# First score passes of an attention stage inside the last feed forward, constant rows loaded once per lot, and some causal masks added by TensorE

## Chip, cores and metric

The kernel runs on one core of a Trainium2 chip. The metric is device time in microseconds (us) of one execution, the median of several runs.

## What is computed

The reference takes x of shape (16, 256, 128), float32, and adds six blocks to it one after the other, each on a layer norm of x:

```python
x = x + 0.5 * ffn0(layernorm(x))      # gated: silu(x w1) * (x w2), two 512x512 gelu layers, 512 -> 128
x = x + attn0(layernorm(x))           # no softmax: (theta phi^T / sqrt(128)) g
x = x + 0.5 * ffn0(layernorm(x))      # the same weights again
x = x + 0.5 * moe(layernorm(x))       # 8 experts, top 2, chosen by each sequence's first row
x = x + attn1(layernorm(x))           # 16 heads of width 8, RoPE, causal softmax over 256 positions
x = x + 0.5 * moe(layernorm(x))
```

## The kernel before, in words

**Order.** All instructions of all engines come from one list of steps. The class `Order` lays it out before the program is built: jobs (generators) call `put` for a step once its inputs are ready by the planned clocks of the engines. `TAKES` (from line 62) holds the planned microseconds of each step on each engine (P TensorE, V VectorE, A ScalarE, G GpSimd, S the sync queue, D a DMA's flight). Among the jobs that can go on, the one with the smallest priority number goes first, and `SHIFT` adds a small number to single jobs. Each engine then runs its steps in the order of the list and waits for semaphores. All DMAs are issued by the SP queue, also in the order of the list.

**Work before the softmax attention.** x is cut into 8 chunks of 512 rows (c = 0 to 7), and the 16 feed forwards (two for each chunk, `QUEUE`) run in two streams, `stream(0)` and `stream(1)`, whose matmuls TensorE takes in turn (`term`, lines 1000 and 1004: a high and a low half of the activations, float32 rounded, 128x512 each). Between the layers ScalarE does silu or gelu (L1457, L1461) and the rounding to the high half (L1468), and VectorE the product (L1292) and the low half (L1297). A stream that finds the queue empty is dead. The first stream to die frees the SBUF that buffers 0 to 2 of the attention use, the second frees the rest: `order.dead` holds their last `down` steps, and `ffns_dead` makes an engine wait for them. In the last feed forward only one stream is alive.

**Preparation.** After a chunk's second feed forward and its experts (`first_moe`), `prepare` turns q and k (L1407, L1411), splits each into three bf16 parts on ScalarE and GpSimd, and `spread` writes them to DRAM (L1669). There are 16 sequences u, two to a chunk. `attend` puts the step `reloc`: SP loads K and Q of a sequence into buffer u % 5 (`KS`, `QS`, L1700). Four rows of each half of KS and two of QS are constants, loaded once (L1690), and `VA` gets a constant pattern (L1686); these loads are the step `ones`, put by the job `opening` (priority 4).

**Attention.** For each sequence there are 8 groups of two heads. `pass1` (job `peaks`) is 4 mask matmuls (L1179) and 4 score matmuls (L1183, L1186) into a pair of PSUM banks, and then one VectorE maximum over 128x768 (L1414). After 8 of them the row maxima are combined (`peak`, L1421), transposed, copied to `MT` (L1427) and sent by SP into two rows of QS (`max_out`, L1705). Then `pass2` (job `probs`) is 4 matmuls (L1213), one exponential over 128x768 on ScalarE (L1553) and one `affine_select` on GpSimd that zeroes the masked half (L1643), and `weigh` multiplies the probabilities by the values (L1227). `fin`, a second `moe` and the stores follow. `probs` starts only when both streams are dead, since its buffer `PB` lies where their data lay. The priority of `peaks` is 5.5 while pass1 is less than `LEAD` = 20 steps ahead of pass2, and 6.5 then; pass2 has 6, the streams 3, their endings 2.85, the work after them 2. `pair` gives a pair of banks only if the planned clock of the reading engine is less than `QUEUED` = 1.0 us ahead of TensorE's. Where the plan shows TensorE idle, `keep` (L1197) fills in small matmuls whose result nobody reads.

Of the kernel before, what the change touches and what calls it, by code (L numbers as in the profile page):

```python
# [7 lines left out]
F32 = mybir.dt.float32  # L8
# [7 lines left out]
S = 256  # L16
# [14 lines left out]
class Step:  # L31
# [68 lines left out]
WEIGH = 6.5  # L100
KEPT = 5
SLOTS = 8
QUEUED = 1.0
LEAD = 20
LONE = 4.0
FILLED = 0.65
# [5 lines left out]
SHIFT = {  # L112
    ("attend", 0): -0.23, ("attend", 1): 0.32, ("attend", 2): -0.07, ("attend", 3): 0.31, ("attend", 11): -0.03,
    ("attend", 12): 0.09, ("attend", 13): 0.54, ("attend", 14): 0.12,
    ("fin", 0): 0.1, ("fin", 4): -0.75, ("fin", 9): -0.69, ("fin", 12): 0.02, ("fin", 14): 0.51,
    ("lone", 7): -0.03,
    ("maxima", 1): -0.03, ("maxima", 4): -0.05, ("maxima", 6): -1.07, ("maxima", 7): -0.15, ("maxima", 8): 0.18,
    ("maxima", 9): 0.02, ("maxima", 12): 0.91, ("maxima", 13): 0.14, ("maxima", 14): 0.54, ("maxima", 15): 0.88,
    ("peaks", 0): -0.31, ("peaks", 4): 0.27, ("peaks", 5): -0.02, ("peaks", 6): 0.13, ("peaks", 7): -0.15,
    ("peaks", 8): -0.11, ("peaks", 9): 0.34, ("peaks", 11): -0.52, ("peaks", 13): -0.26, ("peaks", 15): -0.16,  # L120
    ("probs", 0): 0.09, ("probs", 3): -0.01, ("probs", 5): -0.03, ("probs", 6): -0.39, ("probs", 8): 0.02,
    ("probs", 9): 0.25, ("probs", 10): 0.03, ("probs", 12): 0.24, ("probs", 14): -0.2,
    ("weigher", 0): -0.23, ("weigher", 3): -0.12, ("weigher", 4): 0.01, ("weigher", 8): -0.52,
    ("weigher", 15): -0.24,
}
# [33 lines left out]
class Order:  # L159
# [37 lines left out]
    def put(self, name, **k):  # L197
# [19 lines left out]
        if name == "up" and not self.opened:  # L217
            late = "up_first"
        for i, (eng, us, *way) in enumerate(TAKES[late]):
            if eng == "D":  # L220
                t += us
                continue
            if eng == "P":
                kind = TILES.get(name, "f")
                self.clock["P"] += 0.094 * (kind != self.pe)
                self.pe = kind
            if eng == "A":
                table = "gelu" if name == "tanh" and self.table == "silu" else TABLES.get(name, self.table)
                self.clock["A"] += 1.29 * (table != self.table)
                self.table = table  # L230
            if i or name == "up":
                t = max(t, later - 0.45 * (name == "up"))
            s0 = max((ready if name in BESIDE else t) + HOPS[eng], self.clock[eng])
            if eng == "P":
                self.fill(s0)
                self.idle_from = s0 + us
            self.note(eng, s0, s0 + us, name)
            self.clock[eng] = s0 + us
            t = st.at[eng] = s0 + way[0]
# [55 lines left out]
    def pair(self, eng):  # L295
        while True:
            for b in (4, 2, 0):
                if self.clock[eng] < self.clock["P"] + QUEUED and self.bank[b] is not None and self.bank[b + 1] is not None and self.left(self.bank[b] + self.bank[b + 1]) <= self.clock["P"] + AHEAD:
                    return b
            yield  # L300
# [51 lines left out]
    def next_feed(self, s):  # L352
        if not self.queue:
            return None
        box = {"ffn": self.queue.pop(0)}
        self.add(1, self.begin(box) if box["ffn"] == QUEUE[0] else self.feed(s, box))
        return box
# [5 lines left out]
    def stream(self, s):  # L363
        box = self.next_feed(s)
        while box:
# [67 lines left out]
            self.bank[b] = None  # L433
            self.add(2.85, self.ending(p, c, b, mm))
        if self.first is None:
# [3 lines left out]
    def ending(self, p, c, b, mm):  # L439
        _, free = yield from self.yr.get(self)  # L440
        y = self.put("y", c=c, b=b, src=mm, emptied=free)
        self.bank[b] = [y]
        yield from self.until(y.done)
        b, free = yield from self.sr.get(self)
        bk = self.put("back", c=c, b=b, emptied=free, src=y)
        self.sr.free[b] = [bk]
        self.yr.free[0] = [bk]
        self.add(2, self.first_moe(c, bk) if p else self.attn0(c, bk))

# [69 lines left out]
    def prepare(self, c, src):  # L519
# [31 lines left out]
        for h in range(2):  # L551
            self.add(2.5, self.attend(2 * c + h, a, va), of=("attend", 2 * c + h))
        if c >= NC - 2:
# [22 lines left out]
    def opening(self):  # L576

        for n in range(KEPT):
            m = 1 if n < 3 else 2
            while len(self.dead) < m:  # L580
                yield
            yield from self.until(self.dead[m - 1].done)
            if m == 2:
                self.sr.ids = [6, 7, 5, 4]
            self.qfree[n] = [self.dead[m - 1]]
            self.vfree[n] = [self.put("ones", i=n, x=m, src=self.dead[m - 1])]

    def attend(self, u, prep, va):
# [5 lines left out]
        self.turn["reloc"] += 1  # L594
        self.add(self.lead, self.peaks(u, rl), "h", ("peaks", u))
        while self.vfree[u % KEPT] is None:
# [34 lines left out]
    def probs(self, u, mx):  # L631
# [4 lines left out]
        for i in range(8):  # L636
            while self.pbfree[i % SLOTS] is None:
                yield
            k = yield from self.pair("A")
            p2 = self.put("pass2", u=u, g=i, b=k, src=mx, emptied=self.bank[k] + self.bank[k + 1],  # L640
                          emptied2=self.pbfree[i % SLOTS])
# [91 lines left out]
    def lay(self):  # L733
        self.add(lambda: self.rank(0), self.stream(0))
        self.add(lambda: self.rank(1), self.stream(1))
        self.add(4, self.opening())
        self.run()
# [14 lines left out]
def build(nc, I, out):  # L752
    order = Order()
    with ExitStack() as ctx:
# [81 lines left out]
        QS, KS, VA = {}, {}, {}  # L836
        for n in range(KEPT):
            QS[n] = sb(f"QS{n}", [128, 8, S], BF16)
            KS[n] = sb(f"KS{n}", [128, 8, S], BF16)
            VA[n] = sb(f"VA{n}", [128, 2, NH, 32])  # L840
        PB = sb("PB", [128, SLOTS, 3, 2, 128])
# [13 lines left out]
        s_one = [sem(f"s_one{u}") for u in range(KEPT)]  # L855
        s_far = [sem(f"s_far{u}") for u in range(KEPT)]
        s_qs = [sem(f"s_qs{u}") for u in range(KEPT)]
# [53 lines left out]
        for st in order.steps:  # L911
            if st.name == "down" and st.x:
                k += 1
                nth_down[id(st)] = k


# [81 lines left out]
        def tensor(e, w, steps, lo):  # L998
# [7 lines left out]
            for st in steps:  # L1006
# [163 lines left out]
                elif st.name == "pass1":  # L1170
                    K, Q = KS[u % KEPT], QS[u % KEPT]
                    w.wait_ge(s_qs[u % KEPT], 64 * (u // KEPT + 1))
                    w.wait_ge(s_far[u % KEPT], 64)
                    w.wait_ge(g_c, 6)
# [31 lines left out]
                elif st.name == "pass2":  # L1206
# [3 lines left out]
                    for k in range(2):  # L1210
                        for h in range(2):
                            o = PSA[:, b + h, 0:384].rearrange("p (t q) -> p t q", t=3)
                            t = e.matmul(o[:, 1, :] if k else o[:, 0::2, :],  # L1213
                                         K[64 * h:64 * h + 52, g, 128 * k:128 * k + 128],
                                         Q[64 * h:64 * h + 52, g, 128 * k:256], start=(k == 0), stop=True,
                                         skip_group_check=True)
                    t.then_inc(p_pass2, 1)
                elif st.name in ("weigh", "weighed"):

                    V, a = VA[u % KEPT], g % 2  # L1220
                    w.wait_ge(g_sel, 8 * u + 2 * g + 2)
                    w.wait_ge(a_vexp, u + 1)
# [350 lines left out]
        def gpsimd(e, w):  # L1573
# [4 lines left out]
            for st in order.steps:  # L1578
# [58 lines left out]
                elif st.name == "rest1":  # L1637
                    w.wait_ge(a_cast, 2 * n + 2)
                    e.tensor_tensor(CB[:, g, 2, :], RA[:, 0, :], CB[:, g, 1, :], ALU.subtract).then_inc(g_rest, 1)
                elif st.name == "pass2":  # L1640
                    P = PB[:, n % SLOTS, 0:2, :, :].rearrange("p t l q -> p (t l) q")
# [4 lines left out]
        def sync(e, w):  # L1646
# [25 lines left out]
            for st in order.steps:  # L1672
# [10 lines left out]
                elif st.name == "ones":  # L1683
# [3 lines left out]
                        s_one[st.i], 16)  # L1687
                    for T, a, z in ((KS, 0, 4), (QS, 4, 6)):
                        for h in range(2):
                            e.dma_start(T[st.i][64 * h + 48:64 * h + 48 + z - a, :, :].rearrange(  # L1690
                                "p g s -> p (g s)").bitcast(F32), I["rows"][a:z, :]).then_inc(s_far[st.i], 16)
                elif st.name == "reloc":
                    for side in range(2):
                        w.wait_ge(s_dk[c % 2][side], n_dk * (c // 2 + 1))
                    for s in st.emptied:
                        if s.name == "pass2":
# [108 lines left out]
```

## Time and profile before

| what | value |
|---|---|
| median of 3 runs | 651.84 us (649.85 to 653.08) |
| the profiled execution: its time, its span | 652.16 us, 650.4 us |
| busy share of the span: PE, PEld, DVE, ACT, POOL | 95%, 72%, 75%, 75%, 47% |

PE is TensorE's matmuls, PEld its weight loads, DVE VectorE, ACT ScalarE, POOL GpSimd, SPq the sync engine's DMA issue. Spans of matmuls are modelled and overlap, so a busy PE is not PE at its peak. Idle time of an engine that is not the bottleneck costs nothing. The profile gives for each idle time the instruction whose semaphore came last.

### The profile page before, as it was taken

The numbers are of one execution on the slowest core, as the hardware profiler recorded it, in microseconds if no ns is written. First come the engines' busy times: TensorE is split into PE (matmuls) and PEld (weight loads), VectorE is DVE, ScalarE is ACT, GpSimd is POOL, SyncE is SP. The second block draws the span as 40 slices with busy tenths as digits, with TensorE's granted clock in tenths as the row PEclk, the third lists the DMA queues.
The fourth block names the chain that finished last, engine by engine and source line by source line (L and its number), as shares of the span: only waits on it lengthen the run. The fifth ranks groups of instructions, "written<-read, shape, count | busy, mean of one in ns | idle before, by whom it ended". The sixth has DMA issues, their size and how long they took to land.

```text
span 650.4 us, 14027 instructions
## 1 busy us (share of the span) xinstructions
PE 615.8 (95%) x5210; PEld 466.2 (72%) x5210; DVE 487.3 (75%) x1262; ACT 485.6 (75%) x816; POOL 306.1 (47%) x476
## 2 busy tenths in 40 slices
PE   4899999999999999999999999988999999999997
PEld 3677878888887887888778887765555666656665
DVE  6767566675675777675978768799988989888846
ACT  5799778787887687787788777724777857877892
POOL 1402202321311525222638354576888766767683
PEclk9899999999999999999999999999999999999999
DMA  9300000000000002100002035454444323122002
GB/s 290 109 1 1 1 0 2 1 2 1 1 1 2 0 2 58 40 1 1 1 26 72 2 90 154 155 165 144 122 122 139 113 81 112 55 90 89 10 3 68
DMA packets 41886, 37.80 MB, mean 58 GB/s; under 512 B 2940, under 2 KB 37020, under 8 KB 41816
## 3 DMA queue, kind: packets, MB, share of 16 engines
q1 hardware_dynamic: 41816, 36.87, 18.4%
q8 instruction: 43, 0.70, 0.4%
q14 instruction: 27, 0.22, 0.1%
HBM read 21.92 MB, written 14.68 MB: 56 GB/s over the span
## 4 chain that ended last, share of the span: by engine, by line
PE 66%; DVE 14%; ACT 9%; issue 5%; DMA 2%; POOL 2%; SPq 1%; DVEq 0%; ACTq 0%; POOLq 0%
PE PSA L1000 20%; PE PSA L1004 20%; PE PSA L1227 6%; DVE MX L1414 3%; PE PSA L1019 3%; DVE G L1292 3%; PE PSA L1213 3%; PE PSA L1179 2%; ACT PSA L1461 2%; PE PSA L1156 2%; DMA QS<-MT 2%; ACT G L1457 1%; PE PSA L1163 1%; PE PSA L1186 1%; PE PSA L1197 1%
## 5 line engine op out<-in xcount | busy, mean ns | idle before, releaser
L1000 PE MATMUL PSA<-ah,WH 128*128 128x512 f32 x320 | 130.3, 407 | 0.5 <-DVE G L1292 0.5
L1414 DVE TENSOR_REDUCE MX<-PSA 128x6 f32<-128x768 f32 x128 | 117.9, 949 | 13.8 <-PE PSA L1186 13.1
L1461 ACT ACTIVATE PSA<-PSA,SC 128x512 f32<-128x512 f32 x128 | 84.7, 662 | 55.0 <-PE PSA L1004 54.4
L1004 PE MATMUL PSA<-al,WH 128*128 128x512 f32 x320 | 125.4, 392 | 0.0
L1553 ACT ACTIVATE PB<-PSA 128x768 f32<-128x768 f32 x128 | 98.6, 813 | 28.9 <-PE PSA L1213 27.6
L1000 PE MATMUL PSA<-bh,WH 128*128 128x512 f32 x256 | 104.8, 410 | 2.7 <-DVE G L1292 2.3
L1583 POOL TENSOR_SCALAR VE<-MV 128x4 f32<-128x4 f32 x46 | 11.4, 247 | 194.4 <-DVE MV L1267 194.4
L1004 PE MATMUL PSA<-bl,WH 128*128 128x512 f32 x256 | 100.3, 392 | 0.0
L1643 POOL TENSOR_SCALAR_AFFINE_SELECT PB<-PB 128x512 f32<-128x512 f32 x128 | 80.2, 636 | 36.0 <-ACT PB L1553 34.0
L1297 DVE TENSOR_TENSOR al<-PSA,ah 128x512 fp32r<-128x512 f32 x64 | 44.0, 687 | 52.7 <-ACT ah L1468 52.2
L1000 PEld LDWEIGHTS PSA<-ah,WH 128*128 128x128 f32 x320 | 60.5, 189 | 13.3 <-issue 0.7
L1297 DVE TENSOR_TENSOR bl<-PSA,bh 128x512 fp32r<-128x512 f32 x64 | 44.0, 687 | 33.7 <-ACT bh L1468 33.4
L1004 PEld LDWEIGHTS PSA<-al,WH 128*128 128x128 f32 x320 | 60.5, 189 | 12.1 <-issue 0.7
L1292 DVE SCALAR_TENSOR_TENSOR G<-PSA,SC,G 128x512 f32<-128x512 f32 x64 | 46.7, 747 | 29.6 <-ACT G L1457 22.8
L1597 POOL TENSOR_SCALAR XN<-X,MV,RS 128x128 f32<-128x128 f32 x78 | 62.8, 814 | 3.1
L1000 PEld LDWEIGHTS PSA<-bh,WH 128*128 128x128 f32 x256 | 48.1, 188 | 14.1 <-DVE G L1292 4.9
L1227 PE MATMUL PSA<-PB,VA 128*32 128x256 f32 (+1 forms) x1024 | 55.3, 337 | 2.3 <-DVE X L1317 0.9
L1004 PEld LDWEIGHTS PSA<-bl,WH 128*128 128x128 f32 x256 | 48.2, 188 | 8.9 <-issue 0.2
L1000 PE MATMUL PSA<-XH,WH 128*128 128x512 f32 x128 | 53.3, 416 | 1.4 <-DVE XL L1287 1.4
L1004 PE MATMUL PSA<-XL,WH 128*128 128x512 f32 x128 | 51.1, 399 | 0.0
L1468 ACT ACTIVATE ah<-G 128x512 fp32r<-128x512 f32 x64 | 40.4, 631 | 12.8 <-DVE G L1292 12.7
L1585 POOL TENSOR_TENSOR RS<-VE,MHALF 128x4 f32<-128x4 f32 x46 | 47.9, 1042 | 3.8
(163 smaller groups left out, 1282.7 us busy)
## 6 DMA issues: line engine op xcount, KB each, us to landing
KS<-dk SPq DMA_DIRECT2D x32, 192.0 KB
QS<-dq SPq DMA_DIRECT2D x32, 192.0 KB
dk<-CB SPq DMA_DIRECT2D x16, 192.0 KB, 2.3
dq<-CB SPq DMA_DIRECT2D x16, 192.0 KB, 2.5
VA<-in_ones SPq DMA_DIRECT2D x5, 512.0 KB, 4.7
X<-in_x SPq DMA_DIRECT2D x8, 256.0 KB, 6.8
dk<-CB SPq DMA_DIRECT2D x16, 128.0 KB, 2.0
dq<-CB SPq DMA_DIRECT2D x16, 128.0 KB, 1.9
```

Source lines behind the costliest of these rows:

```text
L1000: e.matmul(o, WH[:, col:col + 128], hi, start=first, stop=False)
L1004: return e.matmul(o, WH[:, col:col + 128], low, start=False, stop=last)
L1227: t = e.matmul(PSA[32 * v:32 * v + 32, b, 128 * k:256], V[:, k, 8 * (g // 2) + 2 * v + a, :], P[:, 1, :] if k else P[:, 0::2, :], start=(k ...
L1292: e.scalar_tensor_tensor(out=G[:, i, :], in0=bank(b), scalar=SC[:, 4 + st.j:5 + st.j], in1=G[:, i, :], op0=ALU.mult, op1=ALU.mult).then_in ...
L1297: e.tensor_tensor(cut(PL_[st.s, dst], st.j), h, cut(PH_[st.s, dst], st.j), ALU.subtract).then_inc(v_lo, 1)
L1414: e.tensor_reduce(MX[:, u % 2, 1:4, :].rearrange("p t (l g) -> p l t g", l=2)[:, :, :, g], PSA[:, b:b + 2, 0:384].rearrange("p l (t k) -> ...
L1461: e.activation(bank(b), bank(b), ACT.Gelu, scale=SC[:, k:k + 1]).then_inc(a_gelu, 1)
L1468: e.activation(cut(PH_[st.s, dst], st.j), G[:, i, :] if g == 0 else bank(b), ACT.Copy).then_inc(a_hi, 1)
L1553: e.activation(PB[:, n % SLOTS, :, :, :].rearrange("p t l q -> p l t q"), PSA[:, b:b + 2, 0:384].rearrange("p l (t q) -> p l t q", t=3), A ...
L1585: e.tensor_tensor(RS[:, i, :], VE[:, i, :], MHALF[:, :], ALU.pow).then_inc(g_rs, 1)
L1597: t = e.tensor_scalar(XN[:, i, j, :], X[:, 4 * c + j, :], MV[:, i, j, 0:1], RS[:, i, j:j + 1], ALU.subtract, ALU.mult)
L1643: e.affine_select(out=P, in_=P, compare_op=ALU.is_ge, fill=0.0, base=0, pattern=[[0, 4], [1, 128]], channel_multiplier=-1).then_inc(g_sel, 1)
```

## The change

`opening` gets priority 1 in place of 4 and works by lots: buffers 0 to 2 when the first stream is dead, 3 and 4 when both are. It puts a new step `rows` first: four DMAs that load the constant rows of all buffers of the lot, from a source repeated by a zero stride (so K and Q of a lot now lie in one tensor `KQ`). The loads into `VA` (`ones`) come after the lot's last `reloc`. `reloc` waits for the dead streams itself. `attend` gets priority 1 in place of 2.5. The job `peaks` of sequences 0 to 2 gets priority 1.5, ahead of the streams, and while fewer than two streams are dead `pair` allows 2.0 us in place of 1.0. A `pass2` is of kind "m" if the planned clock of GpSimd is more than `BEHIND` = 2.0 us ahead of TensorE's: then four more matmuls add the mask (−1e30) to the scores before the exponential, and there is no `affine_select`. `feed`, `ending` and the work after it become jobs that `SHIFT` can name, and all numbers of `SHIFT` are others.

```diff
-    "value": ..., "ones": [("S", 2.4, 2.4), ("D", 6.0)],
+    "value": ..., "rows": [("S", 1.2, 1.2), ("D", 2.0)], "ones": [("S", 0.4, 0.4), ("D", 5.5)],
+    "pass2m": [("P", 0.28, 0.45), ("A", 0.69, 0.81)],
...
+LOTS = (range(3), range(3, KEPT))
-QUEUED = 1.0
+QUEUED = (2.0, 1.0)
+FIRST = (3, 1.5)
+BEHIND = 2.0
...
-                if self.clock[eng] < self.clock["P"] + QUEUED and ...
+                if self.clock[eng] < self.clock["P"] + QUEUED[len(self.dead) > 1] and ...
...
-            self.add(2.5, self.attend(2 * c + h, a, va), of=("attend", 2 * c + h))
+            self.add(1, self.attend(2 * c + h, a, va), of=("attend", 2 * c + h))
...
     def opening(self):
-        for n in range(KEPT):
-            m = 1 if n < 3 else 2
+        for m, lot in ((1, LOTS[0]), (2, LOTS[1])):
             while len(self.dead) < m:
                 yield
             yield from self.until(self.dead[m - 1].done)
             if m == 2:
                 self.sr.ids = [6, 7, 5, 4]
-            self.qfree[n] = [self.dead[m - 1]]
-            self.vfree[n] = [self.put("ones", i=n, x=m, src=self.dead[m - 1])]
+            self.put("rows", i=m - 1, x=m, src=self.dead[m - 1])
+            for n in lot:
+                self.qfree[n] = [self.dead[m - 1]]
+            while self.turn["reloc"] <= lot[-1]:
+                yield
+            for n in lot:
+                self.vfree[n] = [self.put("ones", i=n, x=m, src=self.dead[m - 1])]
...
-        self.add(self.lead, self.peaks(u, rl), "h", ("peaks", u))
+        self.add(FIRST[1] if u < FIRST[0] else self.lead, self.peaks(u, rl), "h", ("peaks", u))
...
+            m = "m" if self.clock["G"] > self.clock["P"] + BEHIND else ""
-            p2 = self.put("pass2", u=u, g=i, b=k, src=mx, ...
+            p2 = self.put("pass2", u=u, g=i, b=k, kind=m, src=mx, ...
...
-        self.add(4, self.opening())
+        self.add(1, self.opening())
...
-        for n in range(KEPT):
-            QS[n] = sb(f"QS{n}", [128, 8, S], BF16)
-            KS[n] = sb(f"KS{n}", [128, 8, S], BF16)
-            VA[n] = sb(f"VA{n}", [128, 2, NH, 32])
+        for k, lot in enumerate(LOTS):
+            KQ[k] = sb(f"KQ{k}", [128, len(lot), 2, 8, S], BF16)
+            for i, n in enumerate(lot):
+                KS[n], QS[n] = KQ[k][:, i, 0, :, :], KQ[k][:, i, 1, :, :]
+                VA[n] = sb(f"VA{n}", [128, 2, NH, 32])
...
# tensor, pass2 (the four score matmuls then end with stop=st.kind != "m")
+                    if st.kind == "m":
+                        for k in range(2):
+                            for h in range(2):
+                                o = PSA[:, b + h, 0:256].rearrange("p (t q) -> p t q", t=2)
+                                t = e.matmul(o[:, :, 64 * k:64 * k + 64], MK[64 * h:64 * h + 64, k, 0, :],
+                                             IM[64 * h:64 * h + 64, k, 64 * k:64 * k + 64].rearrange(
+                                                 "p (o q) -> p o q", o=1).to_broadcast([64, 2, 64]),
+                                             start=False, stop=True, skip_group_check=True)
# tensor, weigh (chosen counts the affine_selects up to a pass2)
-                    w.wait_ge(g_sel, 8 * u + 2 * g + 2)
+                    w.wait_ge(a_prob, 8 * u + 2 * g + 2)
+                    w.wait_ge(g_sel, chosen[8 * u + 2 * g + 1])
# gpsimd
-                elif st.name == "pass2":
+                elif st.name == "pass2" and st.kind != "m":
# sync
-                    for T, a, z in ((KS, 0, 4), (QS, 4, 6)):
+                elif st.name == "rows":
+                    ffns_dead(w, st.x)
+                    for k, a, z in ((0, 0, 4), (1, 4, 6)):
                         for h in range(2):
-                            e.dma_start(T[st.i][64 * h + 48:64 * h + 48 + z - a, :, :].rearrange(
-                                "p g s -> p (g s)").bitcast(F32), I["rows"][a:z, :]).then_inc(s_far[st.i], 16)
+                            T = KQ[st.i][64 * h + 48:64 * h + 48 + z - a, :, k, :, :].rearrange(
+                                "p n g s -> p n (g s)").bitcast(F32)
+                            e.dma_start(T, I["rows"][a:z, :].rearrange("p (o s) -> p o s", o=1).to_broadcast(
+                                [z - a, len(LOTS[st.i]), 4 * S])).then_inc(s_far[st.i], 16)
                 elif st.name == "reloc":
...
+                    ffns_dead(w, 1 + (u % KEPT in LOTS[1]))
```

## Rows read from the trace of the kernel before

**Rows 1.** Windows: length, busy us of PE, PEld, DVE, ACT, POOL, clock, DMA.
```profile
393.00:425.00 32.00, 31.73 (x189) 24.95 (x188) 25.55 (x78) 24.02 (x41) 16.52 (x24) 1.00 0.53 170
425.00:450.00 25.00, 19.92 (x258) 13.45 (x256) 24.01 (x62) 6.27 (x14) 16.49 (x26) 1.00 0.51 159
450.00:617.50 167.50, 160.12 (x2543) 101.25 (x2539) 149.38 (x341) 123.75 (x230) 123.65 (x203) 0.99 0.31 95
617.50:640.00 22.50, 21.42 (x289) 14.21 (x285) 12.56 (x58) 18.59 (x36) 17.37 (x32) 1.00 0.05 14
```

**Rows 2.** The same windows, line L1414 (pass1's maxima) alone.
```profile
393.00:425.00 32.00, 1.90 (x2) 1.00 0.53 170
425.00:450.00 25.00, 13.26 (x15) 1.00 0.51 159
```

**Rows 3.** Groups of instructions, 450 to 617.5 us: busy, mean of one | idle before, releaser.
```profile
L1414 DVE TENSOR_REDUCE MX<-PSA 128x6 f32<-128x768 f32 x112 | 103.3, 949 | 13.8 <-PE PSA L1186 13.1
...
L1643 POOL TENSOR_SCALAR_AFFINE_SELECT PB<-PB 128x512 f32<-128x512 f32 x110 | 68.9, 636 | 33.2 <-ACT PB L1553 31.9
...
L1227 PEld LDWEIGHTS PSA<-PB,VA 128*32 128x32 f32 x880 | 24.2, 110 | 19.9 <-issue 7.3 <-POOL PB L1643 3.6
```

**Rows 4.** Timeline of the SP queue: start, us, line, DMAs.
```profile
393.83 0.69 SPq L1690 DMA_DIRECT2D KS<-in_rows  x2
394.56 0.54 SPq L1690 DMA_DIRECT2D QS<-in_rows  x2
...
398.97 1.65 SPq L1700 DMA_DIRECT2D KS<-dk  x2
400.67 1.43 SPq L1700 DMA_DIRECT2D QS<-dq  x2
...
433.21 1.42 SPq L1700 DMA_DIRECT2D QS<-dq  x2
...
437.68 6.49 SPq L1669 DMA_DIRECT2D dk<-CB  x6
444.22 1.19 SPq L1705 DMA_DIRECT2D QS<-MT  x2
```

**Rows 5.** Timeline of DVE, 412 to 439 us.
```profile
412.67 0.95 DVE L1414 TENSOR_REDUCE MX<-PSA 128x6 f32<-128x768 f32 x1
...
426.53 1.81 DVE L1414 TENSOR_REDUCE MX<-PSA 128x6 f32<-128x768 f32 x2
428.26 0.67 DVE L1302 SCALAR_TENSOR_TENSOR X<-PSA,X 128x512 f32<-128x512 f32 x1
...
437.55 0.20 DVE L1421 TENSOR_REDUCE PK<-MX 128x32 f32<-128x64 f32 x1
```

**Rows 6.** Windows, the first stretch from 400 us on (columns as in rows 1).
```profile
400.00:425.00 25.00, 24.73 (x142) 19.11 (x142) 20.36 (x64) 18.01 (x32) 12.62 (x18) 1.00 0.46 156
```

**Rows 7.** The chain that ended last: the first row maxima on their way.
```profile
444.87 3.90 DMA QS<-MT
```

**Rows 8.** Timeline of PE: two pass1 steps back to back, then the last `back`.
```profile
425.35 0.29 PE L1179 MATMUL PSA<-MK,IM 64*128 64x128 bf16 x4
425.48 0.22 PE L1183 MATMUL PSA<-KS,QS 50*128 50x128 bf16 x2
...
425.64 0.28 PE L1179 MATMUL PSA<-MK,IM 64*128 64x128 bf16 x4
...
426.20 0.65 PE L1051 MATMUL PSA<-IDN,Y 128*128 128x128 f32 x4
```

**Rows 9.** Windows, line L1197 (`keep`) alone: PE, PEld.
```profile
393.00:425.00 32.00, 2.73 (x31) 2.07 (x31) 1.00 0.53 170
425.00:450.00 25.00, 7.51 (x86) 5.33 (x86) 1.00 0.51 159
```

**Rows 10.** Groups of instructions, 617.5 to 640 us.
```profile
L1553 ACT ACTIVATE PB<-PSA 128x768 f32<-128x768 f32 x18 | 13.4, 837 | 0.0
```

More of the change, by code:

```diff
@@ L112 @@
 SHIFT = {
[L113 to L123, printed above, removed]
@@ L124 @@
-    ("weigher", 15): -0.24,
+    ("after", 0, 0): 0.04, ("after", 0, 2): 0.02, ("after", 0, 6): -0.27, ("after", 1, 0): 0.09,
+    ("after", 1, 1): -0.03, ("after", 1, 2): -0.03, ("after", 1, 5): 0.12, ("attend", 0): 0.35,
+    ("attend", 2): 0.22, ("attend", 4): 0.12, ("attend", 6): -0.03, ("attend", 8): -0.58, ("attend", 10): -0.24,
+    ("attend", 11): 0.16, ("attend", 13): -0.09, ("attend", 15): -0.11, ("ending", 0, 0): 0.13,
+    ("ending", 0, 2): -0.01, ("ending", 1, 3): -1.07, ("ending", 1, 4): -0.11, ("ending", 1, 5): 0.04,
@@ new lines @@
+    ("ending", 1, 6): -0.11, ("ending", 1, 7): 0.29, ("feed", 0, 1): -0.61, ("feed", 0, 2): 0.05,
+    ("feed", 0, 3): 0.12, ("feed", 0, 5): -0.1, ("feed", 0, 7): 0.61, ("feed", 1, 1): 0.16, ("fin", 3): 0.94,
+    ("fin", 4): 0.88, ("fin", 6): 0.25, ("fin", 8): 0.17, ("fin", 10): 0.01, ("lone", 6): 0.22,
+    ("maxima", 4): 0.37, ("maxima", 6): 0.06, ("maxima", 11): 0.21, ("maxima", 12): -0.21, ("maxima", 13): -0.41,
+    ("maxima", 14): -0.01, ("maxima", 15): -0.03, ("peaks", 0): -0.44, ("peaks", 10): -0.18, ("peaks", 11): -0.03,
@@ L125 @@
+    ("peaks", 12): 0.11, ("peaks", 13): -0.16, ("peaks", 14): 0.26, ("probs", 0): 0.04, ("probs", 3): -0.26,
+    ("probs", 5): 0.15, ("probs", 7): 0.08, ("probs", 10): 0.04, ("probs", 11): 0.57, ("probs", 12): 0.12,
+    ("probs", 13): 0.26, ("probs", 15): 0.02, ("weigher", 0): -0.5, ("weigher", 2): 0.05, ("weigher", 9): 0.11,
+    ("weigher", 10): -0.08, ("weigher", 12): 0.24, ("weigher", 13): -0.15, ("weigher", 14): 0.12,
+    ("weigher", 15): 0.03,
 }
@@ L218, in put @@
             late = "up_first"
+        if name == "pass2" and st.kind == "m":
+            late = "pass2m"
         for i, (eng, us, *way) in enumerate(TAKES[late]):
@@ L297, in pair @@
             for b in (4, 2, 0):
-                if self.clock[eng] < self.clock["P"] + QUEUED and self.bank[b] is not None and self.bank[b + 1] is not None and self.left(self.bank[b] + self.bank[b + 1]) <= self.clock["P"] + AHEAD:
+                if self.clock[eng] < self.clock["P"] + QUEUED[len(self.dead) > 1] and self.bank[b] is not None and self.bank[b + 1] is not None and self.left(self.bank[b] + self.bank[b + 1]) <= self.clock["P"] + AHEAD:
                     return b
@@ L355, in next_feed @@
         box = {"ffn": self.queue.pop(0)}
-        self.add(1, self.begin(box) if box["ffn"] == QUEUE[0] else self.feed(s, box))
+        self.add(1, self.begin(box) if box["ffn"] == QUEUE[0] else self.feed(s, box), of=("feed", *box["ffn"]))
         return box
@@ L433, in stream @@
             self.bank[b] = None
-            self.add(2.85, self.ending(p, c, b, mm))
+            self.add(2.85, self.ending(p, c, b, mm), of=("ending", p, c))
         if self.first is None:
@@ L447, in ending @@
         self.yr.free[0] = [bk]
-        self.add(2, self.first_moe(c, bk) if p else self.attn0(c, bk))
+        self.add(2, self.first_moe(c, bk) if p else self.attn0(c, bk), of=("after", p, c))
     def normed_T(self, kind, c, src):
@@ L639, in probs @@
             k = yield from self.pair("A")
-            p2 = self.put("pass2", u=u, g=i, b=k, src=mx, emptied=self.bank[k] + self.bank[k + 1],
+            m = "m" if self.clock["G"] > self.clock["P"] + BEHIND else ""
+            p2 = self.put("pass2", u=u, g=i, b=k, kind=m, src=mx, emptied=self.bank[k] + self.bank[k + 1],
                           emptied2=self.pbfree[i % SLOTS])
@@ L836, in build @@
         QS, KS, VA = {}, {}, {}
-        for n in range(KEPT):
-            QS[n] = sb(f"QS{n}", [128, 8, S], BF16)
-            KS[n] = sb(f"KS{n}", [128, 8, S], BF16)
-            VA[n] = sb(f"VA{n}", [128, 2, NH, 32])
+        KQ = [None, None]
+        for k, lot in enumerate(LOTS):
[3 more added lines that the diff above has]
+                VA[n] = sb(f"VA{n}", [128, 2, NH, 32])
         PB = sb("PB", [128, SLOTS, 3, 2, 128])
@@ L855, in build @@
         s_one = [sem(f"s_one{u}") for u in range(KEPT)]
-        s_far = [sem(f"s_far{u}") for u in range(KEPT)]
+        s_far = [sem(f"s_far{k}") for k in range(2)]
         s_qs = [sem(f"s_qs{u}") for u in range(KEPT)]
@@ L914, in build @@
                 nth_down[id(st)] = k
+        chosen, k = [], 0
+        for st in order.steps:
+            if st.name == "pass2":
+                k += st.kind != "m"
+                chosen.append(k)
         x_age, ages, nth_x, k = {}, {}, {}, 0
@@ L1172, in tensor @@
                     w.wait_ge(s_qs[u % KEPT], 64 * (u // KEPT + 1))
-                    w.wait_ge(s_far[u % KEPT], 64)
+                    w.wait_ge(s_far[u % KEPT in LOTS[1]], 64)
                     w.wait_ge(g_c, 6)
@@ L1214, in tensor @@
                                          K[64 * h:64 * h + 52, g, 128 * k:128 * k + 128],
-                                         Q[64 * h:64 * h + 52, g, 128 * k:256], start=(k == 0), stop=True,
+                                         Q[64 * h:64 * h + 52, g, 128 * k:256], start=(k == 0), stop=st.kind != "m",
                                          skip_group_check=True)
+                    if st.kind == "m":
[6 more added lines that the diff above has]
+                                             start=False, stop=True, skip_group_check=True)
                     t.then_inc(p_pass2, 1)
```

2 rows, old and new, of the table TAKES are left out of this document.

## Prediction

> **What bounds the kernel now.** I read the windows first, then the groups of instructions by line in the stretch they point to, then the chain and the timelines of single engines. The windows [rows 1] show three regimes. Until 425 us the feed forwards fill TensorE: 31.73 of 32 us busy, with VectorE at 25.55. From 425 to 450 us TensorE falls to 19.92 of 25 us, of which 7.51 are filler [rows 9], and ScalarE to 6.27, while VectorE has 24.01. From 450 to 617.5 us VectorE is busy for 149.38 of 167.5 us (89%) and TensorE by its busy time for 160.12 (96%), but by its weight loads for 101.25 (60%). After the last maximum the tail of 617.5 to 640 us belongs to ScalarE's exponentials: 18 of them, 13.4 us, with no wait before any [rows 1, 10].
>
> The softmax attention is thus paced by VectorE, above all by 128 maxima (112 of them in the long stretch, 103.3 us, [rows 3]), and its start is a valley: before 425 us only 2 maxima are done [rows 2], the first at 412.67 us [rows 5], although the load of the first K and Q had been issued by 402.1 us [rows 4]. They wait for their turn in the planned order, not for data. ScalarE then has nothing to do until the first sequence's row maxima have been combined (437.55 us, [rows 5]), sent by SP (444.22 us, behind six loads of 6.49 us that began at 437.68 us, [rows 4]) and landed (444.87 + 3.90 = 448.8 us, [rows 7]).
>
> **The change, part by part.** The sum is made against the profiled execution, 652.16 us (span 650.4 us and 1.76 us around it); it lies 0.32 us above the median of 651.84 us.
>
> *First maxima within the last feed forward.* The constant rows of a lot cost four DMAs, 0.69 + 0.54 = 1.2 us of SP's time, and a sequence's K and Q 1.65 + 1.43 = 3.1 us [rows 4]. With the first lot's rows ahead of everything else, the first K and Q would be issued by 393.8 + 1.2 + 3.1, some 398.1 us in place of 402.1, and land by about 402 us if they take the 3.90 us of the MT transfer [rows 7], the nearest row. With priority 1.5 the maxima start there. VectorE's idle time from 400 to 425 us is 25 − 20.36 = 4.6 us [rows 6]; from 393 us on it is 6.45 us [rows 1]; from 425 to 450 us only 1.0 us. As VectorE sets the pace from there to 617 us, what is gained is the idle time that is filled: 0 if the maxima only displace steps of the feed forward, 6.45 at most. I take the value of the stretch in which data are there: **−4.6 us**. On TensorE each pass1 takes 425.64 − 425.35 = 0.29 us [rows 8], 22 of them 6.4 us; they find room in the 0.27 + 2.73 + 5.08 + 7.51 = 15.6 us of idle time and filler that TensorE has from 393 to 450 us [rows 1, 9], so they cost nothing there as long as the streams end before 440 us.
>
> *When pass2 can begin.* It now needs the end of the last stream and no longer the row maxima, which are done before. The stream ended at 425 us. 22 more maxima of 0.9 us (1.81 for two, [rows 5]) put 19.8 us on VectorE, 4.6 of them into idle time, so the end lies between 425 and 440 us; I take 434, since part of what is displaced is preparation and experts, not the stream. The first exponential then comes near 435 us and not at 449. ScalarE is idle for 18.7 of the 25 us of the valley [rows 1], so some ten exponentials can be done early. VectorE's pace hides this until the tail. There 18 are left; 8 belong to the last sequence and cannot come sooner, the other 10 are worth 10 × 0.74 = 7.4 us (13.4/18 each, [rows 10]). The lead rule of 20 steps stands and speaks for no gain, ScalarE's room for all of it; I take not quite half: **−3.3 us**, bounds 0 and −7.4.
>
> *Masks on TensorE.* Four mask matmuls of the same shape in pass1 take 425.48 − 425.35 = 0.13 us [rows 8]. How many pass2 steps take them: GpSimd spends 123.65 − 68.9 = 54.7 us of the long stretch on other work [rows 1, 3], a third, and when it is in such work it is behind; I take a quarter of 128, 32 steps, 4.2 us of TensorE. Bounds are 0 and 128 × 0.13 = 16.6 us. TensorE is 96% busy by matmuls and 60% by weight loads, so I put half on the path: **+2.1 us**. GpSimd loses 32 × 0.636 = 20 us, but the weighing matmuls waited for it for 3.6 us in all [rows 3]; between 0 and −3.6 I take 0. The Trainium skill (Perfetto Trace Analysis, section Identifying the Most-Contended Engine) holds that matmul busy time is a bad measure of TensorE's room and weight-load share a good one; by that the masks would cost nothing and the result would be 642, by the busy share alone 646.
>
> *The new order.* VectorE waited 13.1 us for pass1's matmuls in the long stretch [rows 3]; a better order could save at most that, a worse one lose as much. About a tenth of TensorE's 160 us can move ahead into its 15.6 us of holes, so I take a tenth of VectorE's 18.1 us of idle time there: **−2 us**.
>
> *At no cost.* Eight row loads replace twenty: SP is spared some 12 × 0.31 = 3.7 us, not on the path beyond what is counted above. The `VA` loads come behind the lot's `reloc`; what needs them, the weighing, is at least 10 us later. Were that cover gone, the three loads would delay it by a few us once. `rows` waits for the first dead stream at the head of the SP queue: behind it stand the chunk's `spread` writes, and behind those ScalarE's next cast into `CB`. `attend` at priority 1 moves the `reloc` DMAs ahead of spreads that nobody needs for tens of us. The weighing's new wait on the exponentials, and that of `reloc` on the dead streams, ask for what was waited for already.
>
> Sum: −4.6 − 3.3 + 2.1 − 2 = −7.8, so 644.4 us for an execution like the profiled one and **644 us** against the median.
>
> **Rivals.**
> *Both terms of the start come in full*, 638 us: −6.45 − 7.4 + 2.1 − 2 = −13.8 from 651.84. For it: ScalarE's empty valley. Against it: the lead of 20 is unchanged.
>
> *Hidden anyway*, 651.5 us: the maxima fill VectorE's holes, but the later end of the stream and the masks (4.2 us, all on the path) give it back; pass2 begins little before 449 us. For it: VectorE had only 1 us free after 425 us. Against it: TensorE's filler shows room.
>
> *It does not do what it says*, 653 us: the first maxima come hardly before 412 us, because a pair of neighbouring banks is seldom free beside the stream's own tiles, or because SP stands behind a spread. Only the masks remain, +2.1 and the order's share lost. Against it: the plan has two banks for such a step even now, twice before 425 us [rows 2].
>
> *Slower*, 659 us: the maxima starve the stream. Its steps on VectorE (the product, the low halves) stand behind maxima in one queue; the trace shows the price: the last `back` transposes ended at 426.85 us [rows 8], and the addition that reads them ran at 428.26 us, behind two maxima [rows 5]. The Trainium skill (TensorE: Matmul & The Clock Gate, section on the array's 32×32 sub-arrays) says that ScalarE's and VectorE's queues are strictly in order, which this row bears out. The place is the end of the stream, which gates the second lot of buffers and all of pass2. Sequence 3's K and Q were issued by 434.6 us, 9.6 us after the stream's end [rows 4], and land some 3.9 us later; until then VectorE has only its other work, 24.01 − 13.26 = 10.8 us in the valley [rows 1, 2]. If the maxima of sequences 0 to 2 are done near 440 us, it runs dry at about 451 us; the streams would have to end before 451 − 13.5 = 437.5 us. From there each us costs one: an end at 447 leaves a hole of 9.5, and 652.16 − 4.6 + 2.1 + 9.5 = 659. Against it: priority goes by VectorE's planned clock, at most 2 us ahead.
>
> **How the numbers follow.** My forecast has a chance of 0.62, the full gain 0.13, hidden anyway 0.10, not what it says 0.05, slower 0.10. A measurement of this kernel can tell about 0.5%, 3.3 us, from no change: faster is under 648.6 us (0.62 + 0.13), slower over 655.1 us (0.10), and the rest is the same (0.15). The range goes down to 636 us, the first two terms in full and half the masks' cost gone, and with them 651.84 − 6.45 − 7.4 + 0 − 2 = 636; up to 652 us, both at 0, with the masks and the order against each other. Outside it lie the slower case and little else.
>
> **What would show it.** Right: the first maximum near 402 us and some 20 of them before 430 us; VectorE without idle time from there to 450 us; the first exponential between 430 and 440 us; L1197's filler in the valley a few us less; about 32 fewer `affine_select` instructions; the last maximum between 608 and 612 us and fewer than 18 exponentials behind it. Wrong: a last feed-forward matmul after 438 us with VectorE idle behind it (slower), a first exponential still near 449 us (hidden), a first maximum after 410 us (not what it says), or a long stretch in which VectorE waits more than 13.1 us for TensorE (masks or order mis-sized).

## The result: slower, and the profile after

The changed kernel takes 665.17 us (661.97 to 667.85, 6 runs) against 651.02 us for the kernel before: a ratio of 1.020 (1.017 to 1.023). I had forecast 644 us and faster, with 0.10 for slower. The profiled execution took 663.0 us, its span is 661.3 us, 10.9 us more than before.

The windows of the changed kernel, with the columns and the first three stretches of [rows 1]:

```profile
393.00:425.00 32.00, 22.02 (x158) 15.95 (x156) 18.50 (x43) 17.16 (x29) 9.96 (x15) 0.89 0.53 155
425.00:450.00 25.00, 24.06 (x198) 17.26 (x198) 23.24 (x69) 10.86 (x18) 14.35 (x21) 0.94 0.18 50
450.00:617.50 167.50, 157.93 (x2495) 101.30 (x2489) 147.96 (x346) 117.52 (x219) 106.06 (x169) 0.98 0.36 112
```

A new hole stands in the last feed forward: from 393 to 425 us TensorE has 22.02 us of 32 where it had 31.73, and every other engine falls with it. The valley after 425 us looks filled, with 24.06 us of TensorE in place of 19.92, but in part this is the feed forward itself, which the hole pushed there: its last result is read at 442.2 us (425.5 before). The windows of 10 us show the hole sharply, and a second, smaller one at 460 us:

```profile
400.00:410.00 10.00, 9.83 (x66) 6.71 (x65) 9.42 (x23) 7.20 (x13) 2.20 (x2) 1.00 0.64 187
410.00:420.00 10.00, 4.60 (x40) 3.09 (x38) 2.63 (x6) 1.20 (x3) 2.63 (x7) 0.90 0.68 194
420.00:430.00 10.00, 5.59 (x31) 3.98 (x32) 5.42 (x14) 4.01 (x8) 1.86 (x3) 0.59 0.18 53
...
460.00:470.00 10.00, 5.00 (x60) 2.94 (x59) 4.11 (x13) 2.22 (x5) 4.39 (x8) 0.83 0.48 163
```

When all engines stand still at once, the question is which wait ended last. The waits of the first hole, engine, line, releaser, and us in total, times, longest:

```profile
DVE bl L1330 <- ACT bh L1501: 11.4, 3, 10.8
PEld PSA L1202 <- DVE bl L1330: 10.0, 1, 10.0
...
ACT VA L1578 <- DMA VA<-in_ones: 9.6, 2, 8.8
```

TensorE's next pass1 (L1202) waits for a low half on VectorE, VectorE for the high half on ScalarE, and ScalarE for a DMA. The timeline of ScalarE there:

```profile
410.58 0.60 ACT L1501 ACTIVATE bh<-PSA 128x512 fp32r<-128x512 f32 x1
419.95 0.42 ACT L1578 ACTIVATE VA<-VS 128x256 f32<-128x256 f32 x1 [8.77 <-DMA VA<-in_ones]
421.21 0.72 ACT L1578 ACTIVATE VA<-VS 128x256 f32<-128x256 f32 x2 [0.85 <-DMA VA<-in_ones]
421.84 0.61 ACT L1566 ACTIVATE CB<-RA 128x512 bf16<-128x512 f32 x1
422.36 0.64 ACT L1494 ACTIVATE PSA<-PSA,SC 128x512 f32<-128x512 f32 x1
```

The instruction that stands at the head of ScalarE's queue is `vexp`, a copy of the values into `VA` (line 1545 in the kernel before). It needs the constant pattern that `ones` loads into `VA`. The first weighing, which reads it, runs at 451.6 us, but the feed forward's gelu (L1494) and rounding (L1501) stand behind it. The SP queue and the time of these loads from issue to landing:

```profile
393.41 1.29 SPq L1728 DMA_DIRECT2D KQ<-in_rows  x4
394.82 1.63 SPq L1739 DMA_DIRECT2D KQ<-dk  x2
...
402.82 1.47 SPq L1739 DMA_DIRECT2D KQ<-dq  x2
404.34 1.39 SPq L1719 DMA_DIRECT2D VA<-in_ones  x3
```

```profile
VA<-in_ones SPq DMA_DIRECT2D x5, 512.0 KB, 14.3
```

In the kernel before, the page has 4.7 us in this place. There the three loads went out from 393.35 to 397.2 us, ahead of the K and Q loads (from 398.97 us, [rows 4]), and the first copy found its data there at 402.86 us:

```profile
VA<-in_ones SPq DMA_DIRECT2D x5, 512.0 KB, 4.7
...
393.35 0.43 SPq L1686 DMA_DIRECT2D VA<-in_ones  x1
...
396.83 0.35 SPq L1686 DMA_DIRECT2D VA<-in_ones  x1
...
402.86 0.41 ACT L1545 ACTIVATE VA<-VS 128x256 f32<-128x256 f32 x1
```

In the changed kernel 12 K and Q loads of 192 KB each go ahead of the three, 2.3 MB on the same DMA engines, whose mean share in use is 0.64 and 0.68 in the windows from 400 to 420 us. The last of the three was on its way for 15.8 us (405.30 to 421.13 us in the chain). The planner counts 5.5 us for it (`ones`, D), so it put the copy where the load would have landed by its table.

The hole costs more than its length. TensorE did nothing from 414.6 to 424.4 us. The granted clock fell to 0.50, which is the lower of its two levels, 1.2 GHz, and stayed there while the matmuls began again:

```profile
416.00:418.00 2.00, 0.00 (x0) 0.00 (x0) 0.00 (x0) 0.00 (x0) 0.00 (x0) 0.99 0.39 158
418.00:420.00 2.00, 0.00 (x0) 0.00 (x0) 0.00 (x0) 0.05 (x1) 0.00 (x0) 0.50 0.38 147
...
424.00:426.00 2.00, 1.59 (x12) 1.26 (x12) 2.00 (x4) 0.00 (x0) 0.00 (x0) 0.50 0.42 119
426.00:428.00 2.00, 2.00 (x13) 1.30 (x12) 2.00 (x4) 0.00 (x0) 0.00 (x0) 0.50 0.00 0
```

The second hole is the same wait for the second lot: 4.3 and 1.0 us between 459 and 465 us.

### The profile page after: what moved, and what is told of

It reads as the page before. It is cut to its first block, busy times and chain, and to the rows that moved or that the text cites. A ratio compares the mean times of both kernels' runs of the same rounds, so it can differ in the third digit from the quotient of the medians.

```text
span 661.3 us, 14181 instructions
## 1 busy us (share of the span) xinstructions
PE 619.1 (94%) x5309; PEld 468.2 (71%) x5309; DVE 488.7 (74%) x1262; ACT 486.1 (74%) x816; POOL 284.3 (43%) x437
## 4 chain that ended last, share of the span: by engine, by line
PE 63%; DVE 12%; ACT 10%; issue 5%; DMA 5%; SPq 3%; POOL 1%; POOLq 0%; DVEq 0%; ACTq 0%
PE PSA L1023 18%; PE PSA L1027 18%; PE PSA L1260 6%; DMA VA<-in_ones 4%; PE PSA L1236 3%; DVE MX L1447 3%; PE PSA L1042 3%; DVE G L1325 2%; PE PSA L1202 2%; SPq L1739 2%; ACT PSA L1494 2%; PE PSA L1179 2%; PE PSA L1186 2%; ACT PB L1586 1%; PE PSA L1209 1%
## 5 line engine op out<-in xcount | busy, mean ns | idle before, releaser
L1494 ACT ACTIVATE PSA<-PSA,SC 128x512 f32<-128x512 f32 x128 | 84.7, 662 | 60.8 <-PE PSA L1027 60.2
L1586 ACT ACTIVATE PB<-PSA 128x768 f32<-128x768 f32 x128 | 100.4, 813 | 30.2 <-PE PSA L1236 18.7
L1676 POOL TENSOR_SCALAR_AFFINE_SELECT PB<-PB 128x512 f32<-128x512 f32 x89 | 56.6, 638 | 47.5 <-ACT PB L1586 45.8
L1202 PE MATMUL PSA<-MK,IM 64*128 64x128 bf16 x512 | 36.7, 222 | 17.1 <-DVE bl L1330 9.8
L1501 ACT ACTIVATE ah<-G 128x512 fp32r<-128x512 f32 x64 | 40.4, 631 | 12.8 <-DVE G L1325 12.7
## 6 DMA issues: line engine op xcount, KB each, us to landing
VA<-in_ones SPq DMA_DIRECT2D x5, 512.0 KB, 14.3
```

The source lines that it names most:

```text
L1202: e.matmul(PSA[:, b + h, 0:384].rearrange("p (t k) -> p t k", t=3)[:, 0::2, 64 * k:64 * k + 64], IM[64 * h:64 * h + 64, k, :], MK[64 * h:6 ...
L1494: e.activation(bank(b), bank(b), ACT.Gelu, scale=SC[:, k:k + 1]).then_inc(a_gelu, 1)
L1501: e.activation(cut(PH_[st.s, dst], st.j), G[:, i, :] if g == 0 else bank(b), ACT.Copy).then_inc(a_hi, 1)
L1586: e.activation(PB[:, n % SLOTS, :, :, :].rearrange("p t l q -> p l t q"), PSA[:, b:b + 2, 0:384].rearrange("p l (t q) -> p l t q", t=3), A ...
L1676: e.affine_select(out=P, in_=P, compare_op=ALU.is_ge, fill=0.0, base=0, pattern=[[0, 4], [1, 128]], channel_multiplier=-1).then_inc(g_sel, 1)
```

## The experiments

Theory 1: ScalarE's in-order wait for late `VA` loads, and nothing else, made the kernel slower. Rivals: the early maxima starve the last stream (theory 2, my slower rival); the masks or the new order cost the time (theory 3). All ratios are against the kernel before on the same chip; where a small difference between two kernels counts, these ratios are compared and not the times.

**The loads first.** The `VA` loads of a lot go to its head; all other orders stay.

```diff
 # sync
                 elif st.name == "rows":
                     ffns_dead(w, st.x)
+                    for m in LOTS[st.i]:
+                        e.dma_start(VA[m]..., I["ones"]).then_inc(s_one[m], 16)
-                elif st.name == "ones":
...
```

> The three (then two) VA loads of a lot are issued at the head of the lot, before the constant rows and before any K and Q; every other engine keeps its order. Theory 1 (ScalarE stands in its queue at the first value copy until the VA loads land, 15.8 and 11.8 us after their issue because the K and Q loads are ahead of them on the DMA engines): the waits of 8.8 + 0.85 us near 411 to 421 us and 4.3 + 1.0 us near 459 to 464 us go, and the lowered clock after them; the loads land in about 5 us as before; 644 to 650 us. Theory 2 (the early maxima starve the last feed forward, which would end late anyway): the last feed-forward matmul stays near 440 us and the time at 658 or more. Theory 3 (masks and the new order cost it): 656 or more.

Measured: 650.47 us, 0.999 (0.996 to 1.001). The loads land in 4.9 us and the copies wait for nothing. Theories 2 and 3, which asked for 656 us or more, are out as the main cause. The time lies at the upper edge of theory 1's range. A price seems to show at the other end: TensorE's first pass1 waits for K and Q, which now come behind the `VA` loads.

```profile
PEld PSA L1202 <- DMA KQ<-dq: 3.0, 1, 3.0
```

**The copy late.** DMAs as in the changed kernel; on ScalarE the copies of sequences 0 to 4 are held until the sequence's first exponential.

```diff
 # scalar
+            held, steps = [], []
+            for st in order.steps:
+                if st.name == "vexp" and st.u < KEPT:
+                    held = sorted(held + [st], key=lambda s: s.u)
+                    continue
+                while held and (st.name == "vexp" or st.name == "pass2" and held[0].u <= st.u):
+                    steps.append(held.pop(0))
+                steps.append(st)
-            for st in order.steps:
+            for st in steps:
```

> The DMAs stay as in the changed kernel, so the VA loads land as late as there; only ScalarE's copies into VA of sequences 0 to 4 move down its queue to just before the sequence's first exponential. Theory 1 (in-order wait on ScalarE, nothing else): the same gain as with the loads first, 644 to 650 us, although the loads still take 14 us. If it is the crowded DMA engines themselves that cost (late K and Q, late spreads): 658 or more. Theories 2 and 3: 656 or more.

Measured: 647.38 us, 0.993 (0.991 to 0.996), faster than both kernels and the best of this study. The loads still take 14.0 us. Only the place of five copies in one queue differs from the changed kernel, and 2.7% of the time goes with it. That settles the question between the DMAs' crowd and the wait: late landings alone did not cost the time, the wait for them did. One copy of the second lot still waits 1.0 us. The page's line of the loads, the first exponential, and the windows:

```profile
VA<-in_ones SPq DMA_DIRECT2D x5, 512.0 KB, 14.0
...
437.20 0.81 ACT L1594 ACTIVATE PB<-PSA 128x768 f32<-128x768 f32 x1 [2.17 <-PE PSA L1245]
...
393.00:425.00 32.00, 31.84 (x220) 23.37 (x220) 28.24 (x68) 20.35 (x33) 13.97 (x20) 1.00 0.53 158
425.00:450.00 25.00, 23.84 (x317) 15.26 (x317) 24.55 (x77) 14.39 (x26) 18.25 (x29) 1.00 0.52 149
450.00:617.50 167.50, 161.38 (x2570) 105.47 (x2564) 149.75 (x355) 122.23 (x228) 106.50 (x173) 0.98 0.31 97
617.50:640.00 22.50, 22.37 (x307) 15.27 (x306) 13.67 (x54) 16.67 (x34) 15.04 (x29) 1.00 0.11 32
```

TensorE is full again before 425 us, VectorE's idle time there is 3.8 us in place of 6.45 [rows 1], and the valley holds 14.39 us of ScalarE in place of 6.27.

**The kernel before with its loads late.** One part of the change alone, put into the kernel before.

```diff
 # sync, in the kernel before
                 elif st.name == "ones":
-                    e.dma_start(VA[st.i]..., I["ones"]).then_inc(s_one[st.i], 16)
                 elif st.name == "reloc":
...
+                    for m in {2: (0, 1, 2), 4: (3, 4)}.get(u, ()):
+                        e.dma_start(VA[m]..., I["ones"]).then_inc(s_one[m], 16)
```

> The kernel before with this one part alone: its VA loads move behind the last K and Q load of their lot. Theory 1: ScalarE's copy, placed at 403 us in its queue, waits for loads issued near 407 us that land 12 to 16 us later; a hole of some 12 to 17 us at 403 to 420 us, part of it covered by the valley, 660 to 668 us. Theories 2 and 3: within 2 us of the kernel before.

Measured: 678.48 us, 1.042 (1.039 to 1.045). The direction is theory 1's; the size is above my range. The first wait, 18.5 us, is a little over the 12 to 17 us that I expected, and I had left out the second lot, whose copy waited 12.4 us:

```profile
ACT VA L1545 <- DMA VA<-in_ones: 18.5, 1, 18.5
...
ACT VA L1545 <- DMA VA<-in_ones: 12.4, 1, 12.4
```

**No masks on TensorE, orders kept.** The 39 pass2 steps of kind "m" lose their mask matmuls and get their `affine_select` back, first in the changed kernel, then with the copies late.

```diff
     order = Order()
+    for st in order.steps:
+        if st.name == "pass2":
+            st.kind = ""
```

> The changed kernel with the 39 masks back on GpSimd and none on TensorE, all other orders kept. Theory 1: 39 x 0.13 = 5 us less TensorE work and 39 x 0.64 = 25 us more GpSimd work, near nothing on the path; 661 to 667 us, as the changed kernel. Theory 3 (the masks cost): 655 to 659 us. If the masks help: 668 or more.

> Both edits together: ScalarE's copies moved down as in vexp_late, and all masks back on GpSimd in the order laid for 39 masks on TensorE. Against vexp_late (647.4 us). If the 18 us that no_masks cost over the changed kernel are the price of masks on GpSimd in an order that counts on GpSimd being free, they come again without the stall: 660 to 668 us. If they were the stall and the masks acting together (a late plan met by a late GpSimd): 648 to 654 us. If masks on TensorE cost as in my sum, 645 us.

Measured: 683.06 us, 1.052 (1.047 to 1.058), and 674.23 us, 1.035 (1.031 to 1.040). Both are far above their kernels with masks (665.17 and 647.38), and above the ranges that I had given theory 1 and the misfit of the order (661 to 667 and 660 to 668). TensorE, whose order was laid for a GpSimd with less to do, now waits for it, and its mean clock is lower; the second kernel's wait (450 to 640 us) and long stretch, which had a clock of 0.98 with the masks on TensorE:

```profile
PE PSA L1263 <- POOL PB L1687: 12.2, 7, 3.4
```

```profile
450.00:617.50 167.50, 152.27 (x2211) 96.13 (x2213) 137.82 (x320) 109.13 (x206) 114.35 (x185) 0.92 0.31 97
```

I read this as the price of an order that does not fit its work and not as the worth of the masks; the runs without searched numbers below bear that out.

**Replanned.** Three kernels in which the planner lays a new order, with the numbers of `SHIFT` as in the changed kernel: no masks and the copies late; no priority for the first sequences and the copies late; and the changed kernel with the true flight of the loads in the planner's table.

```diff
-BEHIND = 2.0
+BEHIND = 1e9
```

```diff
-FIRST = (3, 1.5)
+FIRST = (0, 1.5)
```

```diff
-    ..., "ones": [("S", 0.4, 0.4), ("D", 5.5)],
+    ..., "ones": [("S", 0.4, 0.4), ("D", 15.5)],
```

> vexp_late with BEHIND so large that no mask goes to TensorE, the order laid out again by the planner with the same SHIFT. If the masks on TensorE are worth something in themselves, 2 to 6 us above vexp_late: 649 to 654 us. If the 18 us are only the price of an order that does not fit its masks: 645 to 648 us, as vexp_late. If it is far worse (660 or more), the numbers of SHIFT do not carry over and it says nothing of the masks.

> vexp_late with the priority 1.5 of the first three sequences taken away (they go by the lead rule as before), the order laid out again with the same SHIFT. If the early maxima bring the gain of vexp_late over the kernel before (3.8 us): first maximum near 412 us, 650 to 653 us. If the gain comes from the earlier loads and the tail alone: 646 to 649 us.

> The changed kernel with one number of the planner's table: a VA load is counted with 15.5 us of flight in place of 5.5; no hand edit of any engine's order. The planner should then place ScalarE's copies some 10 us later and lay the rest around them. If theory 1 is whole, the holes go: 644 to 650 us. If the copies still wait 4 us or more in ScalarE's queue, the number is not the only fault: 655 or more.

Measured: 661.37 us, 1.017 (1.015 to 1.020); 673.29 us, 1.037 (1.033 to 1.040); 667.05 us, 1.026 (1.023 to 1.030). The third is a miss that teaches: no copy waits for its load any more and the last feed forward's result is read at 431.1 us in place of 442.2, so the hole is gone, yet the kernel is no faster. The first pass2 now waits for its maxima, and the first exponential comes at 451.3 us (437.2 with the copies late).

```profile
PE PSA L1236 <- DMA KQ<-MT: 6.2, 1, 6.2
...
440.52 1.20 SPq L1744 DMA_DIRECT2D KQ<-MT  x2
...
441.18 9.49 DMA KQ<-MT
```

It is the old mistake in a new place. VectorE had copied the maxima to `MT` by 435.1 us, but the new order lets SP issue the second lot first, its rows, K, Q and `VA`, from 431.08 to 440.5 us; the maxima went out behind it and took 9.49 us to land, where they took 3.90 before [rows 7]. With the copies late SP issued them at 431.95 us, ahead of the second lot. This is read from the traces; no run separates it from the rest of the new order.

None of the three tells what its part is worth, since `SHIFT` was searched for another plan. That called for a common footing.

**Without the searched numbers.** `SHIFT` emptied, in the kernel before, in the kernel with the copies late, and in that without masks.

```diff
-SHIFT = { ... }
+SHIFT = {}
```

> The kernel before with all numbers of SHIFT taken away, the order laid out by the planner alone. If the searched numbers are worth what the replanned runs suggest (14 to 26 us), 660 to 672 us. If the search is worth little and the replanned runs were slow for another reason: 650 to 654 us.

> vexp_late with all numbers of SHIFT taken away. On the same footing as before_unshifted it shows the structure without the search. If early passes and masks are a gain in themselves: 3 us or more under before_unshifted. If the gain of vexp_late is the new search: equal to it within 3 us or above it.

> The same with no mask on TensorE: the masks' worth on an order that was searched for neither. If the masks relieve a GpSimd that is late: 2 to 8 us above late_unshifted. If they only cost TensorE time: 1 to 4 us under it.

Measured: 659.40 us, 1.013 (1.008 to 1.019); 652.21 us, 1.001 (0.998 to 1.003); 652.26 us, 1.001 (0.999 to 1.004). On equal footing the structure, with the copies late, is worth 1.0134 − 1.0007 = 1.27%, 8.3 us, give or take some 4 us by the two intervals; the masks are worth nothing that these runs can tell, 0.05% with some 0.36% either way, which is 2.3 us. The search is worth 1.3% (8.7 us) to the kernel before and 1.0007 − 0.9932 = 0.75% (4.9 us) to the new structure. And numbers searched for another plan are worse than none in the one kernel that has both runs: without masks and with the copies late, 1.017 with them and 1.001 with none.

**The masks twice.** In the best kernel each set of mask matmuls is issued twice; the masked scores get −2e30.

```diff
-                        for k in range(2):
+                        for k in (0, 1, 0, 1):
```

> vexp_late with each of the 39 sets of mask matmuls issued twice (the same masked positions get -2e30), all orders kept: the price of masks on TensorE by doubling it. 39 x 0.13 = 5.1 us more TensorE time. My sum put half of it on the path: 2.5 us, 650 us. If TensorE has room by its weight loads: within 1 us of vexp_late (647.4). If TensorE's 96% busy time is the bound: 652 us or more.

Measured: 649.63 us, 0.998 (0.996 to 1.000), 2.3 us more than the kernel with single masks by medians and 2.9 us by the ratios, of 5.1 us added to TensorE. The two intervals all but touch, so the size is rough: by them it lies between 0.9 and 5 us.

## Why the prediction was wrong

**The step that failed** stands under "At no cost": "The `VA` loads come behind the lot's `reloc`; what needs them, the weighing, is at least 10 us later. Were that cover gone, the three loads would delay it by a few us once." Both halves are wrong. What first needs the loads is not the weighing but ScalarE's copy, and in the trace of before that copy stands at 402.9 us, in the middle of the last feed forward. I asked when the data are used and not at which place of an in-order queue somebody waits for them. And I gave the loads no flight of their own: I moved them behind 2.3 MB of other loads, where they took 14.3 us in place of 4.7. So a wait that the sum put at nothing cost ScalarE 8.77 + 0.85 us for the first lot and 4.3 + 1.0 us for the second, with TensorE idle and then at its lower clock. Moving the place of five copies gives back 17.8 us (665.17 − 647.38); late loads alone cost the kernel before 4.2%. Theory 1 stands, by an edit in either direction.

I had weighed the in-order rule of the Trainium skill (TensorE: Matmul & The Clock Gate, section on the array's 32×32 sub-arrays) for VectorE alone. ScalarE's timeline above shows the same for its queue: a gelu whose matmuls had ended by 413.2 us stood until 422.36 us behind copies that nobody needed yet.

**The slower rival** had the right place (the last stream, its end late, pass2 gated) and the wrong cause. The stream ended late by the hole: its last result is read at 442.2 us in the changed kernel and at 430.7 us with the copies late. What is left over the 425.5 us of the kernel before, 5.2 us, is all that the maxima ahead of it and the other changes of order cost it together; I had taken 9. No starving of the stream is needed to explain the time.

**The terms of the sum**, read from the kernel without the stall:
- *First maxima early.* They came earlier, but less than I said: the first at 407.2 us in place of 412.7 (I said 402), 8 maxima by 425 us in place of 2, and 11 by 430 us where I wanted some 20. VectorE's idle time from 393 to 425 us fell by 2.7 us, not by 4.6. And the gain did not come out where I had priced it: the last maximum stands at 614.0 us in both kernels, where I said 608 to 612.
- *Pass2 earlier.* The first exponential at 437.2 us in place of 449.2, near the 435 forecast. The last maximum did not come earlier, but the tail behind it is 4.0 us shorter (646.4 − 614.0 against 650.4 − 614.0). I had −3.3, by fewer exponentials left, which hardly happened: 18 stand behind 615.1 us, where 19 did before. What shrank is the work of all engines behind 615.1 us, by 2.6 us on TensorE, 1.6 on VectorE, 3.1 on ScalarE and 4.0 on GpSimd. VectorE had done some of its other work sooner: without its maxima it is busy for 148.10 − 98.58 = 49.5 us from 450 to 615.1 us, and was for 148.59 − 102.75 = 45.8, though 1.8 of these 3.7 us only moved there from before 450 us. Which engine's share sets the shorter tail is not shown.
- *Masks.* 39 steps where I took 32. Doubling them costs 2.3 to 2.9 us, where half of 5.1 was forecast. So the middle between busy time (all of it) and weight loads (none) agrees with the run, but with a size known only to 0.9 to 5 us this is no sharp test. By the Trainium skill (Perfetto Trace Analysis, Identifying the Most-Contended Engine) the share of weight loads tells TensorE's room; that alone was too kind to TensorE here. GpSimd's relief, which I had put at 0 between 0 and −3.6, may give the cost back: without the searched numbers the net is 0 within 2.3 us.
- *The new order.* Not confirmed: I had −2. The search brought the new structure 4.9 us and the old one 8.7, so on balance it took back 3.8 of the structure's 8.3. By the intervals this 3.8 has some 4.4 us either way, so that its sign is likely but not shown. The new numbers were also searched for a plan that counts 5.5 us for the `VA` loads.

Structure −8.3 and search +3.8 make −4.5, which is the best kernel's 0.9932 by construction and no second measurement. Without the stall the forecast would have been right in sign, with −7.8 us where some −4.4 are measured, and its range would have held; but with the last maximum unmoved this would have been luck in part. What part of the 8.3 belongs to the early passes and what part to the loads was not separated, since the run meant for it went by an order that did not fit.

## What to carry to other kernels

When a load is moved, look for every instruction that waits for it and at its place in its engine's queue: one copy that nobody needs yet stops all that stands behind it. Count a load's landing from the loads ahead of it on the DMA engines, not from its time alone. An order searched for one plan can be worth less than none on another, so compare parts with the search taken out of both.

## What was not expected of the hardware

- The same 512 KB load lands 4.7 us after its issue at the head of its lot and 14.3 us behind 2.3 MB of K and Q loads.
- A hole of 9.8 us on TensorE leaves the granted clock at 0.50 until 428 us, 3.6 us after the matmuls have begun again: a 128x512 matmul takes 0.80 us there and 0.39 us at 412 us. The hole is paid for twice in this way. With the masks back on GpSimd in an order not laid for it, the clock averages 0.92 over the long stretch, against 0.98.
